# Routed expert blocks: the up product with the weights stationary, ScalarE copying each block's weights

## The chip, the cores and the metric

The kernel runs on one core of a Trainium2 chip. The metric is the time of one execution on the device in microseconds (us), as the median of several runs; lower is better.

## The reference

One decoder layer on x of shape (4, 512, 256), all in float32. Each of its three parts is fed by a layer norm and added to x: a selective state-space block of 2 layers, cross attention with 16 heads over a context of 512 rows, and a feed-forward part with 8 routed experts and a shared one. The change touches the last:

```python
xt = x.reshape(T, D)                      # T = 2048, D = 256
probs = softmax(xt @ Wg)                  # 8 experts
topv, topi = top_k(probs, 2); topv = topv / sum(topv)
cw = zeros((T, E)).at[arange(T)[:, None], topi].set(topv)
h = gelu(einsum('td,edf->tef', xt, Wu))   # F = 512
y = einsum('tef,efd->ted', h, Wd)
moe = einsum('ted,te->td', y, cw)
shared = gelu(xt @ W1) @ W2
out = x + shared + moe
```

## The kernel before

It is written engine by engine: for each stage a function per engine (pe_ffn, act_ffn, dve_ffn, pool_ffn, sp_ffn) issues that engine's instructions in a fixed order, and semaphores tie them together. An engine stops at a wait, and all that is queued behind it stops too. The state-space stage takes the span to about 1050 us and attention to about 1410 us; the feed-forward stage is the rest.

In the feed-forward stage the normed tokens xm are stored to x_hat in DRAM and transposed into xn; the router's logits, the softmax and the top two follow. Each of the 4096 choices of a token gets a row in one of NBLK = 39 blocks of 128 rows, and each block belongs to one expert. block_at holds for each block where the weights of its expert begin in w_up and w_down. The shared expert is worked out for all tokens, the first batch's output before the routed blocks and the others behind them (L1562).

The routed blocks run through this loop, in turns j:

- POOL gathers the 128 rows of a block from x_hat into xb (6 buffers) by an indirect DMA (pool_fetch, L1745), and scatters finished rows to y_choice by another (pool_send, L1751). Its queue holds fetch(j + 5), then send(j), then fetch(j + 6). A send waits until DVE has scaled the block.
- PE (L1552 to L1561) in turn j: the up product of block j (pe_up, L1501), the transposes of the rows of block j + 2 (pe_rows, L1495), the transposes of the hidden block j - 1 (pe_hidden_turn, L1510) and the down product of block j - 2 (pe_down, L1516). In pe_up the rows xt, 128x128 for each half of the model's width, are the stationary operand and 512 columns of w_up the moving one, so that the hidden block comes out with its rows on partitions. The down product needs the inner layer on partitions, hence the transposes.
- ACT applies Gelu from PSUM to hb (L1589).
- DVE in turn j: it scales the down product of block j - 3 by the gates into yb (dve_block_out, L1700), copies the transposed rows of j + 2 to xt (dve_rows, L1692) and the transposed hidden block of j - 1 to ht (dve_hidden, L1696).

In PSUM the up product has banks 0 and 1, the hidden transposes 2 and 3, the down product 4 and 5, the row transposes 6 and 7. When all scatters have landed, SP loads y_choice back (into w_up's place), DVE adds the two choices of every token to the residual (L1715), and the output is stored.

A float32 matmul leaves two weight loads and two matmuls in the trace, a transpose one of each; these are called passes here.

Of the kernel before, what the change touches and what calls it, by code (L numbers as in the profile page):

```python
# [8 lines left out]
ACT = mybir.ActivationFunctionType  # L9
# [6 lines left out]
P = 128  # L16
# [8 lines left out]
EXPERTS = 8  # L25
# [7 lines left out]
NBLK = 39  # L33
# [14 lines left out]
def build(nc, d, out):  # L48
# [14 lines left out]
    with ExitStack() as ctx:  # L63
# [5 lines left out]
        def sb(c, name, shape, dt=F32):  # L69
            return c.enter_context(nc.sbuf_tensor(name, shape, dt))  # L70
# [1267 lines left out]
        with ExitStack() as fc:  # L1338
# [28 lines left out]
            block_at = sb(fc, "block_at", [P, NBLK], I32)  # L1367
            NXB, NXT, NHT, NYB = 6, 3, 3, 4
            xb = sb(fc, "xb", [P, NXB, D])
            xt = sb(fc, "xt", [P, NXT, KD, P])  # L1370
            hb = sb(fc, "hb", [P, 2, F])
            ht = sb(fc, "ht", [P, NHT, FT, P])
# [25 lines left out]
            NHID, OUT0, RANKS, LOGITS = 4, 4, 6, 7  # L1398
            U0, H0, T0 = 0, 2, 6
            NTR = B * KD  # L1400
# [11 lines left out]
            fetched = [sem(f"fetched{n}") for n in range(NXB)]  # L1412
            xt_full, xt_out, up_full, up_act, ht_full, ht_out, y_full2, y_out2 = (
                sem(n) for n in ("xt_full", "xt_out", "up_full", "up_act", "ht_full", "ht_out", "y_full2", "y_out2"))
            sent = [sem(f"sent{n}") for n in range(NYB)]
# [84 lines left out]

            def pe_up(j, at):  # L1501
                pe.wait_ge(xt_out, j + 1)
                if j == 0:
                    pe.wait_ge(ld_up, 16 * EXPERTS)
                    pe.wait_ge(hid_act, NTR + NSH)
                for kt in range(KD):
                    m = pe.matmul(psum[:, U0 + j % 2, :], xt[:, j % NXT, kt, :], w_up[:, bass.ds(at + kt * F, F)], start=kt == 0, stop=kt == KD - 1)  # L1507
                m.then_inc(up_full, 1)

            def pe_hidden_turn(j):  # L1510
                pe.wait_ge(up_act, j + 1)
                for ft in range(FT):
                    m = pe.transpose(psum[:, H0 + j % 2, ft * P:(ft + 1) * P], hb[:, j % 2, ft * P:(ft + 1) * P], ident[:])
                m.then_inc(ht_full, 1)

            def pe_down(j, at):  # L1516
                pe.wait_ge(ht_out, j + 1)
                if j == 0:
                    pe.wait_ge(ld_down, 16 * EXPERTS)
                    pe.wait_ge(out_added, NEAR_OUT)  # L1520
                for ft in range(FT):
                    m = pe.matmul(out_bank(j)[:, 0:D], ht[:, j % NHT, ft, :], w_down[:, bass.ds(at + ft * D, D)], start=ft == 0, stop=ft == FT - 1)  # L1522
                m.then_inc(y_full2, 1)

            def pe_ffn():
# [26 lines left out]
                for j in range(NBLK + 2):  # L1552
                    if j < NBLK:
                        at[j] = pe.value_load(block_at[0:1, j:j + 1], min_val=0, max_val=(EXPERTS - 1) * KD * F)
                        pe_up(j, at[j])
                    if j + 2 < NBLK:
                        pe_rows(j + 2)
                    if 1 <= j <= NBLK:
                        pe_hidden_turn(j - 1)
                    if j >= 2:  # L1560
                        pe_down(j - 2, at[j - 2])  # L1561
# [3 lines left out]
            def act_expert_logits(b):  # L1565
                act.wait_ge(lg_full, b + 1)
                act.copy(lgT[:, b, :], psum[0:EXPERTS, OUT0 + b % 2, :]).then_inc(lg_act, 1)

            def act_ffn():
# [10 lines left out]
                for b in range(B):  # L1580
                    for ft in range(FT):
                        q = NTR + b * FT + ft
                        act.wait_ge(hid_full, q + 1)
                        if b == B - 1 and ft == 0:
                            act.wait_ge(hat_set, 16 * B)
                        act.activation(hs[b][:, ft, :], hid_bank(q), ACT.Gelu).then_inc(hid_act, 1)
                for j in range(NBLK):
                    act.wait_ge(up_full, j + 1)
                    act.activation(hb[:, j % 2, :], psum[:, U0 + j % 2, :], ACT.Gelu).then_inc(up_act, 1)  # L1589

# [101 lines left out]
            def dve_rows(j):  # L1692
                dve.wait_ge(xt_full, j + 1)
                dve.tensor_copy(xt[:, j % NXT], psum[:, T0 + j % 2, 0:D].rearrange("p (k c) -> p k c", k=KD)).then_inc(xt_out, 1)

            def dve_hidden(j):  # L1696
                dve.wait_ge(ht_full, j + 1)
                dve.tensor_copy(ht[:, j % NHT], psum[:, H0 + j % 2, :].rearrange("p (k c) -> p k c", k=FT)).then_inc(ht_out, 1)

# [23 lines left out]
            def dve_ffn():  # L1723
# [9 lines left out]
                for j in range(NBLK + 3):  # L1733
                    if j >= 3:
                        dve_block_out(j - 3)
                    if j + 2 < NBLK:
                        dve_rows(j + 2)
                    if 1 <= j <= NBLK:
                        dve_hidden(j - 1)
                for b in range(NEAR, B):  # L1740
# [145 lines left out]
```

## Time and profile before

| what | value |
|---|---|
| median of 3 runs | 1656.67 us |
| lowest, highest | 1651.78, 1661.15 us |
| profiled execution | 1661.1 us |
| its span, first to last instruction | 1659.6 us |
| its mean granted TensorE clock | 0.965 |
| instructions | 24075 |

How to read it: the span is what the hardware profiler sees of one execution, and the profiled execution's own time is 1.5 us more. Starts and lengths are in us from the span's start, ns where marked. PE is TensorE's matmul, PEld its weight load, PEldq and PE's queue its sequencer, DVE VectorE, ACT ScalarE, POOL GpSimd, SP SyncE. Matmuls are pipelined and their ends are modelled, so the distance from start to start tells more than a duration. L1507 is line 1507 of the kernel.

### The profile page before, as it was taken

What the parts mean: (1) busy time and instruction counts of PE and PEld (TensorE: products, weight loads), DVE (VectorE), ACT (ScalarE), POOL (GpSimd) and SP (SyncE); (2) the same over time, 40 slices, a digit from 0 to 9 for tenths busy, and PEclk for the clock granted to TensorE, in tenths of its full rate; (3) what the DMA queues carried; (4) which work ended last, traced back from release to release, by engine and by line L of the source; (5) the groups of instructions that cost most, each with busy time, mean ns of one, the idle gap of its engine ahead of it and who ended that gap; (6) DMA issues with size and microseconds to landing.
All of it is one profiled execution on the core that took longest, in us unless ns stands there. A gap on an engine that the chain in (4) does not pass through costs nothing.

```text
span 1659.6 us, 24075 instructions
## 1 busy us (share of the span) xinstructions
PE 1518.3 (91%) x8994; PEld 1149.5 (69%) x8994; DVE 1181.8 (71%) x1912; ACT 826.8 (50%) x1183; POOL 1001.4 (60%) x818
## 2 busy tenths in 40 slices
PE   4689999999999999999999897768979897999997
PEld 2478878978978879879888897524434343477776
DVE  4389989879879889889888789467667672333334
ACT  3656556656656556656556444105546556411110
POOL 1469878979979969969969987651303000034441
PEclk8999999999999999999999999969989999999999
DMA  4000100101100100101101120245323200612225
GB/s 152 19 26 27 52 26 27 52 26 53 52 26 27 52 26 27 52 26 36 43 26 66 51 102 1 64 83 120 61 55 54 49 1 1 261 38 65 66 64 168
DMA packets 38050, 92.27 MB, mean 56 GB/s; under 512 B 9136, under 2 KB 21936, under 8 KB 33456
## 3 DMA queue, kind: packets, MB, share of 16 engines
q1 hardware_dynamic: 29328, 73.16, 13.9%
q0 software_dynamic: 7584, 16.53, 3.9%
q10 hardware_dynamic: 1024, 1.05, 0.3%
q8 instruction: 73, 1.20, 0.3%
q14 instruction: 41, 0.34, 0.1%
HBM read 64.36 MB, written 9.57 MB: 45 GB/s over the span
## 4 chain that ended last, share of the span: by engine, by line
PE 75%; DVE 14%; issue 4%; ACT 3%; POOL 1%; SPq 1%; DMA 1%; DVEq 0%; ACTq 0%; POOLq 0%
PE psum L491 23%; PE psum L472 10%; PE psum L423 5%; DVE uw L534 4%; PE psum L1522 4%; PE psum L1507 4%; DVE hst L632 4%; PE psum L1091 4%; PE psum L1073 2%; PE psum L452 2%; PE psum L1057 2%; ACT pT L1146 2%; PE psum L1452 2%; PE psum L1017 2%; PE psum L447 1%
## 5 line engine op out<-in xcount | busy, mean ns | idle before, releaser
L801 POOL TENSOR_TENSOR hst<-hst,cb 128x512 f32<-128x512 f32 x399 | 510.8, 1305 | 126.8 <-DVE hst L632 125.8
L632 DVE TENSOR_TENSOR_SCAN hst<-dA,hst,psum 128x256 f32<-128x256 f32 x399 | 277.0, 729 | 79.7 <-PE psum L491 78.0
L632 DVE TENSOR_TENSOR_SCAN hst<-dA,psum 128x256 f32<-128x256 f32 x399 | 253.0, 669 | 40.4 <-ACT dA L743 20.6
L491 PE MATMUL psum<-filt,uT 128*128 128x172 f32 (+1 forms) x1536 | 269.3, 312 | 11.3 <-DVE hst L632 9.1
L491 PE MATMUL psum<-filt,c_early 128*128 128x172 f32 (+1 forms) x1536 | 269.3, 312 | 9.1 <-DVE hst L632 5.9
L491 PEld LDWEIGHTS psum<-filt,c_early 128*128 128x128 f32 x1536 | 233.5, 192 | 47.0 <-issue 20.8
L491 PEld LDWEIGHTS psum<-filt,uT 128*128 128x128 f32 x1536 | 232.4, 191 | 40.4 <-DVE hst L632 15.2
L743 ACT ACTIVATE dA<-delta,alog 128x512 f32<-128x512 f32 x256 | 176.9, 721 | 152.4 <-DVE hst L632 121.5
L743 ACT ACTIVATE dA<-xres,alog 128x512 f32<-128x512 f32 x256 | 177.0, 720 | 127.6 <-DVE hst L632 100.0
L472 PE MATMUL psum<-ident,hst 128*128 128x128 f32 x1596 | 239.9, 274 | 0.0
L1218 DVE TENSOR_REDUCE nmax<-psum 128x2 f32<-128x1024 f32 x128 | 154.9, 1221 | 80.1 <-PE psum L1057 79.8
L472 PEld LDWEIGHTS psum<-ident,hst 128*128 128x128 f32 x1596 | 199.7, 141 | 1.1
L1146 ACT ACTIVATE pT<-psum 128x1024 f32<-128x1024 f32 x128 | 127.9, 1024 | 82.3 <-PE psum L1077 80.9
L801 POOL TENSOR_TENSOR w_early<-w_early,cb 128x512 f32<-128x512 f32 x113 | 145.9, 1307 | 29.9 <-DVE w_early L632 29.7
L1748 POOL DMA_INDIRECT xb<-x_hat,origin x39 | 37.9, 972 | 189.5 <-DVE c_early L1690 178.0
L423 PE MATMUL psum<-xnT,w_early 128*128 128x512 f32 x256 | 124.6, 614 | 4.0 <-DVE uw L534 2.8
L1301 POOL DMA_DIRECT2D qk<-part x72 | 34.5, 489 | 151.7 <-PE psum L1077 131.6
L780 POOL TENSOR_TENSOR filt<-toep,bcol 128x2064 f32<-128x2064 f32 x32 | 116.9, 3654 | 0.0
L632 DVE TENSOR_TENSOR_SCAN w_early<-dA,w_early,psum 128x256 f32<-128x256 f32 x113 | 80.1, 729 | 25.6 <-PE psum L491 25.3
L1589 ACT ACTIVATE hb<-psum 128x512 f32<-128x512 f32 x39 | 23.3, 598 | 145.7 <-PE psum L1507 129.0
L1057 PE MATMUL psum<-qk 64*128 64x512 f32 x256 | 59.9, 470 | 38.2 <-DMA qk<-part 15.4
L1754 POOL DMA_INDIRECT y_choice<-yb,goal x39 | 38.6, 989 | 79.7 <-DVE yb L1706 79.7
(217 smaller groups left out, 2313.4 us busy)
## 6 DMA issues: line engine op xcount, KB each, us to landing
cb<-c_rows SPq DMA_DIRECT2D x32, 1024.0 KB, 4.6
qk<-part SPq DMA_DIRECT2D x120, 64.0 KB, 2.5
qk<-part POOLq DMA_DIRECT2D x72, 64.0 KB, 4.8
w_up<-up_dram SPq DMA_DIRECT2D x8, 512.0 KB, 7.8
w_down<-down_dram SPq DMA_DIRECT2D x8, 512.0 KB, 14.0
w_up<-y_choice SPq DMA_DIRECT2D x8, 512.0 KB, 7.9
xm<-x_dram SPq DMA_DIRECT2D x4, 512.0 KB, 7.8
w_early<-w_in_dram SPq DMA_DIRECT2D x2, 1024.0 KB, 5.5
```

The source lines that it names most:

```text
L423: i = pe.matmul(bk, w_in[:, kt, m8 * P:(m8 + 1) * P], xnT[:, kt, :], start=kt == 0, stop=kt == KD - 1)
L472: m = pe.matmul(psum[:, Y0 + et, t * P:(t + 1) * P], hst(i)[:, t * P:(t + 1) * P], ident[:], start=n == 0 and t == 0, stop=n == NSTATE - 1 ...
L491: m = pe.matmul(bk[:, :, t0:t0 + width], uT[k % 2][:, c, et * P:(et + 1) * P], filt[:, f % 2, c, n2:n2 + 2, 0:width], start=True, stop=True)
L534: i = dve.scalar_tensor_tensor(out=dst, in0=bk[:, 0:S - late], scalar=w_cv[:, l, j, tap:tap + 1], in1=dst, op0=ALU.mult, op1=ALU.add)
L632: dve.tensor_tensor_scan(h[:, t0:t0 + HS], dA[:, st % NDA, t0:t0 + HS], bank("v", i)[:, n * HS:(n + 1) * HS], h[:, t0 - 1:t0] if t0 else 0 ...
L743: act.activation(dA[:, a % NDA, :], delta[k % 2][:, et, :], ACT.Exp, scale=alog[:, k // B, et, n:n + 1]).then_inc(decay_done, 1)
L780: pool.tensor_tensor(filt[:, f % 2], toep[:, :].unsqueeze(1).unsqueeze(1).to_broadcast([P, NCH, GN, QC]), bcol[:, k % 2, :, g * GN:(g + 1) ...
L801: pool.tensor_tensor(h, h, cb[:, q % 2, state_of(i)[1] % GN, :], ALU.mult).then_inc(g_done, 1)
L1057: m = pe.matmul(o[:, e, :], qk[k0:k0 + KR, b % 2, 0, j, half, t * P:(t + 1) * P], qk[k0:k0 + KR, b % 2, 1, j, half, :], start=True, stop=T ...
L1091: m = pe.matmul(psum[i * HROW:(i + 1) * HROW, PV, :], vt[:, cp, kv, c0:c0 + HROW], pT[:, (m0 + i // 2) % NPT, i % 2, :], start=kv == 0, st ...
L1146: act.activation(pT[:, m % NPT], pair(u, "score", s), ACT.Exp, scale=HDIM ** -0.5).then_inc(pair_act, 1)
L1218: dve.tensor_reduce(nmax[:, u % 2, t, 2 * j:2 * j + 2], pair(u, "max", r), AX.X, ALU.max, negate=True).then_inc(pair_dve, 1)
```

## The change

The up product is turned round: the expert's weights become the stationary operand, 128x128 at a time (4 tiles of the inner layer by 2 halves of the model's width), and the 128 rows of the block the moving one. It comes out with the inner layer on partitions, as the down product wants it. The transposes of the hidden block (pe_hidden_turn) and DVE's copy (dve_hidden) are gone, and ACT's Gelu writes ht itself. For each block ACT reads block_at into a register and copies the 128x1024 weights of its expert from w_up to one of 4 fixed places, wu, which lie in xn's memory (act_weights); it does so for block j + 1 ahead of the Gelu of block j. The up product now has 4 PSUM banks (NUB = 4). New waits: the up product for the copy and for the Gelu of 4 blocks before, the down product for DVE's scaling of 2 blocks before, the Gelu for the down product of 3 blocks before, dve_rows for the up product of 3 blocks before.

```diff
--- before.py
+++ after.py
@@ -1365,10 +1365,10 @@
             passed = sb(fc, "passed", [P, NBLK, EXPERTS])
             blockf = sb(fc, "blockf", [P, NBLK])
             block_at = sb(fc, "block_at", [P, NBLK], I32)
-            NXB, NXT, NHT, NYB = 6, 3, 3, 4
+            NXB, NXT, NHT, NYB, NWU = 6, 3, 3, 4, 4
             xb = sb(fc, "xb", [P, NXB, D])
+            wu = xn[:].rearrange("p b k s -> p (b k s)").rearrange("p (n c) -> p n c", n=NWU)
             xt = sb(fc, "xt", [P, NXT, KD, P])
-            hb = sb(fc, "hb", [P, 2, F])
             ht = sb(fc, "ht", [P, NHT, FT, P])
             yb = sb(fc, "yb", [P, NYB, D])
             NSEND = 2 * TOPK * NT
@@ -1396,7 +1396,8 @@
             token_no = route_c[:, 576:576 + NT]
 
             NHID, OUT0, RANKS, LOGITS = 4, 4, 6, 7
-            U0, H0, T0 = 0, 2, 6
+            U0, NUB, T0 = 0, 4, 6
+            wu_set = sem("wu_set")
             NTR = B * KD
             NSH = B * FT
             NGO = TOPK * NT
@@ -1410,8 +1411,8 @@
                 sem(n) for n in ("choice_dve", "gate_dve", "place_dve", "hot_dve", "goal_dve", "blocks_set", "goals_set"))
             hat_set = sem("hat_set")
             fetched = [sem(f"fetched{n}") for n in range(NXB)]
-            xt_full, xt_out, up_full, up_act, ht_full, ht_out, y_full2, y_out2 = (
-                sem(n) for n in ("xt_full", "xt_out", "up_full", "up_act", "ht_full", "ht_out", "y_full2", "y_out2"))
+            xt_full, xt_out, up_full, ht_out, y_full2, y_out2 = (
+                sem(n) for n in ("xt_full", "xt_out", "up_full", "ht_out", "y_full2", "y_out2"))
             sent = [sem(f"sent{n}") for n in range(NYB)]
             y_loaded, y_summed = [sem(f"y_loaded{b}") for b in range(B)], sem("y_summed")
 
@@ -1498,23 +1499,23 @@
                     m = pe.transpose(psum[:, T0 + j % 2, kt * P:(kt + 1) * P], xb[:, j % NXB, kt * P:(kt + 1) * P], ident[:])
                 m.then_inc(xt_full, 1)
 
-            def pe_up(j, at):
+            def pe_up(j):
                 pe.wait_ge(xt_out, j + 1)
+                pe.wait_ge(wu_set, j + 1)
                 if j == 0:
-                    pe.wait_ge(ld_up, 16 * EXPERTS)
                     pe.wait_ge(hid_act, NTR + NSH)
-                for kt in range(KD):
-                    m = pe.matmul(psum[:, U0 + j % 2, :], xt[:, j % NXT, kt, :], w_up[:, bass.ds(at + kt * F, F)], start=kt == 0, stop=kt == KD - 1)
+                if j >= NUB:
+                    pe.wait_ge(ht_out, j - NUB + 1)
+                for ft in range(FT):
+                    for kt in range(KD):
+                        m = pe.matmul(psum[:, U0 + j % NUB, ft * P:(ft + 1) * P], wu[:, j % NWU, kt * F + ft * P:kt * F + (ft + 1) * P], xt[:, j % NXT, kt, :],
+                                      start=kt == 0, stop=kt == KD - 1)
                 m.then_inc(up_full, 1)
-
-            def pe_hidden_turn(j):
-                pe.wait_ge(up_act, j + 1)
-                for ft in range(FT):
-                    m = pe.transpose(psum[:, H0 + j % 2, ft * P:(ft + 1) * P], hb[:, j % 2, ft * P:(ft + 1) * P], ident[:])
-                m.then_inc(ht_full, 1)
 
             def pe_down(j, at):
                 pe.wait_ge(ht_out, j + 1)
+                if j >= 2:
+                    pe.wait_ge(y_out2, j - 1)
                 if j == 0:
                     pe.wait_ge(ld_down, 16 * EXPERTS)
                     pe.wait_ge(out_added, NEAR_OUT)
@@ -1552,11 +1553,9 @@
                 for j in range(NBLK + 2):
                     if j < NBLK:
                         at[j] = pe.value_load(block_at[0:1, j:j + 1], min_val=0, max_val=(EXPERTS - 1) * KD * F)
-                        pe_up(j, at[j])
+                        pe_up(j)
                     if j + 2 < NBLK:
                         pe_rows(j + 2)
-                    if 1 <= j <= NBLK:
-                        pe_hidden_turn(j - 1)
                     if j >= 2:
                         pe_down(j - 2, at[j - 2])
                 for b in range(NEAR, B):
@@ -1565,6 +1564,12 @@
             def act_expert_logits(b):
                 act.wait_ge(lg_full, b + 1)
                 act.copy(lgT[:, b, :], psum[0:EXPERTS, OUT0 + b % 2, :]).then_inc(lg_act, 1)
+
+            def act_weights(j):
+                at = act.value_load(block_at[0:1, j:j + 1], min_val=0, max_val=(EXPERTS - 1) * KD * F)
+                if j >= NWU:
+                    act.wait_ge(up_full, j - NWU + 1)
+                act.copy(wu[:, j % NWU, :], w_up[:, bass.ds(at, KD * F)]).then_inc(wu_set, 1)
 
             def act_ffn():
                 for b in range(B):
@@ -1584,9 +1589,16 @@
                         if b == B - 1 and ft == 0:
                             act.wait_ge(hat_set, 16 * B)
                         act.activation(hs[b][:, ft, :], hid_bank(q), ACT.Gelu).then_inc(hid_act, 1)
+                act.wait_ge(blocks_set, 1)
+                act.wait_ge(ld_up, 16 * EXPERTS)
+                act_weights(0)
                 for j in range(NBLK):
+                    if j + 1 < NBLK:
+                        act_weights(j + 1)
                     act.wait_ge(up_full, j + 1)
-                    act.activation(hb[:, j % 2, :], psum[:, U0 + j % 2, :], ACT.Gelu).then_inc(up_act, 1)
+                    if j >= NHT:
+                        act.wait_ge(y_full2, j - NHT + 1)
+                    act.activation(ht[:, j % NHT], psum[:, U0 + j % NUB, :].rearrange("p (k c) -> p k c", k=FT), ACT.Gelu).then_inc(ht_out, 1)
 
             def dve_route_choose():
                 lg = psum[:, LOGITS, 0:NT * EXPERTS].rearrange("p (t x) -> p t x", x=EXPERTS)
@@ -1691,11 +1703,9 @@
 
             def dve_rows(j):
                 dve.wait_ge(xt_full, j + 1)
+                if j >= NXT:
+                    dve.wait_ge(up_full, j - NXT + 1)
                 dve.tensor_copy(xt[:, j % NXT], psum[:, T0 + j % 2, 0:D].rearrange("p (k c) -> p k c", k=KD)).then_inc(xt_out, 1)
-
-            def dve_hidden(j):
-                dve.wait_ge(ht_full, j + 1)
-                dve.tensor_copy(ht[:, j % NHT], psum[:, H0 + j % 2, :].rearrange("p (k c) -> p k c", k=FT)).then_inc(ht_out, 1)
 
             def dve_block_out(j):
                 dve.wait_ge(y_full2, j + 1)
@@ -1735,8 +1745,6 @@
                         dve_block_out(j - 3)
                     if j + 2 < NBLK:
                         dve_rows(j + 2)
-                    if 1 <= j <= NBLK:
-                        dve_hidden(j - 1)
                 for b in range(NEAR, B):
                     dve_outputs_late(b)
                     dve_choices(b - 1)
```

## Rows read from the trace of the kernel before

**Rows 1.** The page's first part: busy time, share of span, instructions of each engine

```profile
PE 1518.3 (91%) x8994; PEld 1149.5 (69%) x8994; DVE 1181.8 (71%) x1912; ACT 826.8 (50%) x1183; POOL 1001.4 (60%) x818
```

**Rows 2.** Busy time of each engine in 40 us of the routed blocks

```profile
core 0: us, PE busy (x) PEld busy (x) DVE busy (x) ACT busy (x) POOL busy (x), PEclk, DMA share, GB/s
1480.00:1520.00 40.00, 40.00 (x179) 28.29 (x178) 15.52 (x29) 5.98 (x10) 19.68 (x20) 1.00 0.19 63
```

**Rows 3.** The chain of waits from 1440 us to the end, by line

```profile
by line: PE psum L1522 30.6%; PE psum L1507 30.5%; PE psum L1436 9.4%; PE psum L1513 7.7%; PE psum L1452 6.8%; PE psum L1498 3.7%; PE psum L1492 3.2%; PE psum L1462 3.2%; DVE xres L1715 1.7%; issue 0.9%; DVE xres L1730 0.3%; DVE xt L1694 0.
```

**Rows 4.** Timeline, one turn: start us, us, engine, line, operation, count [idle before]

```profile
1520.09 1.88 PE L1507 MATMUL psum<-w_up,xt 128*128 x4
1520.29 0.48 DVE L1706 TENSOR_SCALAR yb<-psum,c_early 128x256 f32<-128x256 f32 x1 [1.04 <-PE psum L1522]
...
1521.05 0.99 POOL L1754 DMA_INDIRECT y_choice<-yb,goal  x1 [1.83 <-DVE yb L1706]
...
1521.80 0.38 PE L1498 MATMUL psum<-ident,xb 128*128 128x128 f32 x2
...
1522.02 0.60 PE L1513 MATMUL psum<-ident,hb 128*128 128x128 f32 x4
...
1522.35 0.97 POOL L1748 DMA_INDIRECT xb<-x_hat,origin  x1 [0.30 <-PE psum L1498]
...
1522.46 1.89 PE L1522 MATMUL psum<-w_down,ht 128*128 x8
1522.66 0.69 DVE L1698 COPY ht<-psum 128x512 f32<-128x512 f32 x1
...
1524.19 1.88 PE L1507 MATMUL psum<-w_up,xt 128*128 x4
...
1525.87 0.20 PEld L1498 LDWEIGHTS psum<-ident,xb 128*128 128x128 f32 x2 [0.63 <-DMA xb<-x_hat,origin]
```

**Rows 5.** Gathered rows xb, 1480 to 1620 us: time to landing, and PE's waits

```profile
DMA to landing us min/median/max: 2.7/2.7/3.3
...
PEld psum L1498 <- DMA xb<-x_hat,origin: 2.4, 5, 0.6
```

**Rows 6.** Timeline of PE where float32 matmuls of 128 columns stand

```profile
1440.96 0.38 PE L1486 MATMUL psum<-member,route_c 128*128 128x128 f32 x2
1441.18 0.39 PE L1487 MATMUL psum<-member,route_c 128*128 128x128 f32 x2
1441.40 1.02 PE L1452 MATMUL psum<-xn,raw 128*128 128x512 f32 x2
```

**Rows 7.** L1492, 78 columns: its weight loads (ns min/median/max), then its matmuls' timeline

```profile
L1492 PEld LDWEIGHTS psum<-c_early,w_early x64: 186/192/192, 1454.9 to 1462.1; 128*128 128x128 f32 x64
...
1455.14 7.27 PE L1492 MATMUL psum<-c_early,w_early 128*128 128x78 f32 x64
```

**Rows 8.** Groups of ScalarE: busy us, mean ns | idle before

```profile
L1146 ACT ACTIVATE pT<-psum 128x1024 f32<-128x1024 f32 x128 | 127.9, 1024 | 82.3 <-PE psum L1077 80.9
L743 ACT ACT_TABLE_LOAD x19 | 24.4, 1283 | 0.3
...
L1574 ACT COPY xn<-psum 128x512 f32<-128x512 f32 x8 | 4.5, 588 | 3.5 <-PE psum L1531 3.5
```

**Rows 9.** PE's queue reads a block's register: ns min/median/max, first and last start

```profile
L1554 PEldq TENSOR_LOAD <-block_at x39: 297/301/491, 1468.4 to 1618.2; - x39
...
L1554 PEldq SEQ_ASSERT  x39: 18/18/32, 1469.2 to 1618.8; - x39
```

**Rows 10.** Timeline where the routed blocks begin

```profile
1470.56 1.98 PE L1507 MATMUL psum<-w_up,xt 128*128 x4 [0.76 <-DVE xt L1694]
...
1472.57 0.60 ACT L1589 ACTIVATE hb<-psum 128x512 f32<-128x512 f32 x1 [16.63 <-issue]
```

**Rows 11.** Timeline of the tail

```profile
1644.00 7.07 PE L1436 MATMUL psum<-raw,xm 128*128 128x256 f32 x32
...
1651.71 4.87 DVE L1715 TENSOR_TENSOR xres<-xres,w_up 128x1024 f32<-128x1024 f32 x4
```

## Prediction

> **What bounds the kernel now.** The core's totals come first: TensorE is busy for 91% of the span, more than any other engine [rows 1]. That is an average over stages, so the next view is the table by stretch, for the stage that the change touches, the 39 routed blocks [rows 2]. In 40 us there PE is busy 40.00 us, POOL 19.68, DVE 15.52 and ACT 5.98, at a granted clock of 1.00 (2.4 GHz). A busy PE can still hide waits, as the ends of its matmuls are modelled, so two more views are needed. The chain of waits from 1440 us on says the same: nearly all of its 220 us are PE lines, the up product L1507 30.5%, the down product L1522 30.6%, the hidden transposes L1513 7.7% and the row transposes L1498 3.7%, against 0.9% of issue [rows 3]. The timeline of one turn of the loop shows how little is between them [rows 4]: the up product starts at 1520.09, the row transposes at 1521.80, the hidden ones at 1522.02, the down product at 1522.46 and the next up product at 1524.19. A turn is 4.10 us and divides into 1.71 (up, 4 passes), 0.22 (2 transposes), 0.44 (4 transposes) and 1.73 (down, 8 passes). I read starts, not durations: a pass of 512 columns has its next start after 0.43 us and the transposes follow at 0.11 us. So each microsecond taken out of PE's stream in a turn comes off the stage, until something else is late.
>
> What could be late next is the gather of rows. After the down product's end (1520.09) follow DVE's scaling (1520.29), POOL's scatter (1521.05) and, behind it in the same queue, POOL's gather of the rows that PE transposes in the next turn (1522.35) [rows 4]. It lands 2.7 us after its issue, 3.3 at worst [rows 5], say 1525.05, and PE needs it at the end of the next up product, 1525.90. Five gathers in 140 us (34 blocks) came after PE's weight load could have started, 2.4 us in all and 0.6 the longest; the one in this turn let the load start at 1525.87, which is still before the up product's end [rows 4, 5].
>
> **The change, part by part.**
>
> *Hidden transposes and DVE's copy go.* 4 passes, 0.44 us from 1522.02 to 1522.46 [rows 4], for 39 blocks: 17.0 us off the path. The chain gives the same: 7.7% of 220 us is 16.9, 0.109 a pass [rows 3]. DVE loses its copy L1698 (0.69 us a turn, rows 4), and ACT's hop through hb becomes a direct write of ht. Neither is late now, so both count as nothing.
>
> *The up product is turned round.* Now xt is the stationary operand: 2 matmuls of 512 columns, each two passes (x4 in rows 4), 1.71 us. Afterwards the weights are: 4 x 2 matmuls of 128 columns, 16 passes, each with its own load of 128x128 weights. Columns times passes are the same, 2048; the question is what a pass of 128 columns costs when each needs a new load. L1486 and L1487 are exactly such matmuls, float32, 128x128 weights, 128 columns, two passes each: they start at 1440.96 and 1441.18, and the next line at 1441.40, so 0.110 us a pass [rows 6]. Bounds: the transposes' 0.109 [rows 3], and the 64 passes back to back of L1492, which move only 78 columns and so are held by the load, 7.27 us or 0.1136 a pass [rows 7]. I take 0.110: 16 x 0.110 = 1.76 us, 0.045 more than now, 39 blocks +1.8 us; bounds +1.1 and +4.0.
>
> The Trainium skill, "TensorE: Matmul & The Clock Gate", section "Part 3: Packing small matmuls — row/col tiling", says that a weight load overlaps matmuls in flight only when it goes to other row groups. The trace disagrees: these loads use all 128 rows, and they follow each other at 0.11 us though one lasts 0.19 [rows 7]. By that rule the sum would turn positive, which is the last rival below.
>
> *The row transposes and the down product stay.* 0.22 and 1.73 us. The new turn is 1.76 + 0.22 + 1.73 = 3.71 us.
>
> *ScalarE copies weights.* Per block one read of the block's place into a register and one copy of 128x1024 from SBUF to SBUF. The copy is not in the trace; nearest are the activation of 128x1024 from PSUM, 1.02 us, and the table load of 1.28 us as a far upper end [rows 8]. I take 1.0. The same register read on PE's queue spans 1468.4 to 1469.2, some 0.8 us and up to 1.1 with what follows it [rows 9]. With the Gelu (0.60, rows 10) and 0.2 for a wait, ACT needs 2.9 of 3.71 us a turn, and the copy for block j+1 is queued ahead of the Gelu of block j, right behind the Gelu of j-1, so it is finished some 2.2 us after the up product of j-1 and due 3.71 + 0.22 + 1.73 = 5.66 us after it. Cover: 0.8 us of idle ACT a turn, and that lead of 3.4 us. What waits behind the copy on ACT is the Gelu, whose result PE wants two turns later. Cost nothing in the steady loop. At the start the first two turns have no down product (1.98 us each), and the copy for block 2 is issued after the Gelu of block 0: 1472.57 + 1.0 + 1.0 + 0.2 = 1474.8, against an up product due at 1470.56 + 3.96 = 1474.52 [rows 10]. That is +0.3 us once (bounds 0 and 1). The copies for blocks 0 and 1 are hidden: ACT is idle before block 0's Gelu at 1472.57 for 16.63 us [rows 10].
>
> *Added waits.* The down product of j waits for DVE's scaling of j-2, the up product for the Gelu of j-4, DVE's xt copy for the up product of j-3. Each event lies about a turn or more back (the scaling is done 0.7 us after its product, rows 4), so nothing. PE still reads its block register for the down product; the read (0.30 us, rows 9) and what depends on it must fit under the down product's 1.73 us, which it does.
>
> *The gather comes closer.* Unchanged chain: from the down product's end to landing 1525.05 - 1520.09 = 4.96 us, some 5.05 until PE can act, and 5.78 in the late case (1525.87 - 1520.09). What PE leaves it shrinks from 4.10 + 1.71 = 5.81 to 3.71 + 1.76 = 5.47 us. The median still fits, by 0.4; a late one costs 0.3. A wait of 0.63 now would cost 0.31, so about 0.3 of each stays hidden: 2.4 - 5 x 0.3 = 0.9 us together. Bounds: nothing, and 39 x 0.31 = 12 us if each landed like the worst.
>
> *Head and tail.* Before block 0, PE is held by the chain to the gathered rows, which stays. In the tail PE's late shared outputs run on to about 1651, and only then come DVE's last sums at 1651.71 [rows 11]; the scatter's and y_back's chain starts from the last down product too. So the saving shifts the whole tail.
>
> **Sum.** -17.0 + 1.8 + 0.3 + 0.9 = -14.0 us. The profiled execution took 1661.1 us (span 1659.6), so its like would be 1647.1. It is the slowest of the runs shown, 4.4 us above their median; against the median, 1656.67 - 14.0 = 1642.7 us, -0.84%.
>
> **The rivals.**
>
> *The gather sets the turn.* If landings move up by 0.4 us or more (gather and scatter share one queue, and now come every 3.7 us), the turn is landing time less the up product: with the late 5.78 each time, 5.78 - 1.76 = 4.02 us, a gain of 0.08 x 39 = 3 us, 1654. Halfway, 5.6: 3.84 a turn, gain 10. For it: five late ones of 34. Against it: the median is 2.7 us and so is the least, so the bulk is tight; POOL is at work 20 of 40 us and stays below 22 [rows 2, 5]. Chance of a gain under 8 us through this or dearer passes: 0.12.
>
> *ScalarE becomes the bound (slower).* If copy and Gelu each needed a table load, ACT would have 2 x 1.28 + 1.0 + 0.6 + 1.0 + 0.2 = 5.4 us a turn, and it decides from 3.71 on: 39 x (5.4 - 4.1) = +51, 1708 us. Against it: L1574's copies come after Sqrt work and show no load at their line, while loads stand with the Exp of L743 [rows 8]. The Trainium skill, "ScalarE: Activation LUTs", "Table sets: the hidden batching unit", says that copy is in every set; the trace agrees. Chance 0.04.
>
> *Weight loads don't overlap (slower).* A pass is then load (0.19, rows 7) and stream (0.11, rows 6), 0.30 us: up 4.8 us, turn 6.75, +103 us, 1760. Rows 6 and 7 speak against it; what is new is only that 16 stand together and that the weights differ from those there. Chance 0.02.
>
> *The change does less than it says.* PE might grant less clock in the stage, or its queue might run dry in the stream of short passes. 64 short passes ran at 0.11 us each, and the routed stage with its short transposes has a clock of 1.00 [rows 2, 7]. Chance 0.02, somewhere near no change.
>
> **How the numbers follow.** Forecast 0.80 (gains of 10 to 17 us): 1642.7. The runs before lie 9.4 us apart, so a median can miss by some 4. The range goes from a gain of 17 with 4 of scatter (1636) to a gain of 7 with 4 of scatter (1654). About 0.5%, 8.3 us, is what a measurement can tell from no change. Faster: 0.80; within 0.5%: 0.13; slower: 0.07.
>
> **What would show it.** Turns of 3.7 us between down products; L1513 and L1698 gone; up passes at 0.11 us start to start; a copy of about 1.0 us on ACT with no table loads in the loop; PE's weight load for the row transposes waiting for the gather in a few turns only, by about 0.3 us; the tail the same length. Wrong would be: a wait for the gather in most turns, passes over 0.12 us, or PE waiting for the weights' copy after block 2.

## The result, and the profile after

| | before | changed |
|---|---|---|
| median of 7 runs | 1653.58 us | 1644.12 us |
| lowest to highest | 1651.78 to 1661.15 | 1641.13 to 1647.13 |
| ratio of changed to before | | 0.993 (95%: 0.9914 to 0.9946) |
| span of the profiled execution | 1659.6 us | 1641.0 us |
| routed stage in it, first up product to late shared outputs | 159.63 us | 149.83 us |
| from there to the end of the span | 29.4 us | 29.4 us |

The change makes the kernel faster, by 0.7% or 11.6 us (8.9 to 14.2); the two medians lie 9.5 us apart. The two profiled spans differ by 18.6 us, but half of that is not the change's: block 0's up product starts at 1470.56 before [rows 10] and at 1461.83 after, and ahead of it both kernels do the same work. In the twelve kernels below that start lies anywhere between 1461.3 and 1472.0 us. So the stage is what to compare between traces, and the ratio over many runs for the whole. The stage's ends after, in the timeline:

```profile
1461.83 2.05 PE L1511 MATMUL psum<-xt,xn 128*128 128x128 f32 x16 [0.68 <-DVE xt L1708]
...
1611.66 4.70 PE L1437 MATMUL psum<-raw,hs_own 128*128 128x256 f32 x21
```

The late shared outputs start at 1611.66, against 1630.19 before. 1611.66 - 1461.83 = 149.83 us, 9.8 less than before, which lies within the ratio's interval.

The page's totals and the 40 us inside the stage (the views of rows 1 and 2; columns as there):

```profile
PE 1497.7 (91%) x9306; PEld 1169.9 (71%) x9306; DVE 1154.9 (70%) x1873; ACT 866.9 (53%) x1222; POOL 1001.0 (61%) x818
```

```profile
core 0: us, PE busy (x) PEld busy (x) DVE busy (x) ACT busy (x) POOL busy (x), PEclk, DMA share, GB/s
1480.00:1520.00 40.00, 39.07 (x268) 36.49 (x267) 9.51 (x21) 16.61 (x21) 20.13 (x21) 1.00 0.21 67
```

PE stays the bound; of 40 us it now stands still for 0.93, ACT's busy time rises from 5.98 to 16.61 us with the copies, DVE's falls from 15.52 to 9.51, and the clock stays at 1.00 [rows 2]. The chain of waits from 1435 us on (the view of rows 3) has a new entry:

```profile
by line: PE psum L1511 27.9%; PE psum L1523 26.9%; DMA xb<-x_hat,origin 12.8%; PE psum L1437 10.1%; PE psum L1453 5.8%; PE psum L1499 4.7%; PE psum L1493 3.4%; PE psum L1463 3.4%; DVE xres L1725 1.8%; issue 1.3%; DVE xres L1740 0.3%; DVE xt
```

The hidden transposes' 7.7% are gone, and the gathered rows, which did not show before, hold 12.8%: the chain runs through a gather wherever PE waited for one. A turn without such a wait (the view of rows 4):

```profile
1469.80 1.95 PE L1511 MATMUL psum<-xt,xn 128*128 128x128 f32 x16
1470.01 0.48 DVE L1716 TENSOR_SCALAR yb<-psum,c_early 128x256 f32<-128x256 f32 x1 [1.31 <-PE psum L1523]
1470.78 1.00 POOL L1762 DMA_INDIRECT y_choice<-yb,goal  x1 [7.77 <-DVE yb L1716]
...
1471.59 0.38 PE L1499 MATMUL psum<-ident,xb 128*128 128x128 f32 x2
1471.79 0.60 ACT L1601 ACTIVATE ht<-psum 128x512 f32<-128x512 f32 x1 [2.05 <-PE psum L1511]
1471.81 1.89 PE L1523 MATMUL psum<-w_down,ht 128*128 x8
...
1472.08 0.98 POOL L1756 DMA_INDIRECT xb<-x_hat,origin  x1 [0.30 <-PE psum L1499]
1472.42 1.04 ACT L1572 COPY xn<-w_up 128x1024 f32 x1
1473.54 1.95 PE L1511 MATMUL psum<-xt,xn 128*128 128x128 f32 x16
```

From 1469.80 to 1473.54 a turn is 3.74 us by these rows, 3.73 in the median: up product 1.79, row transposes 0.22, down product 1.73. The Gelu starts 0.20 us after the up product's end and the copy of the weights directly behind it. And a turn with a wait:

```profile
1477.27 1.95 PE L1511 MATMUL psum<-xt,xn 128*128 128x128 f32 x16
...
1479.25 0.60 ACT L1601 ACTIVATE ht<-psum 128x512 f32<-128x512 f32 x1 [2.06 <-PE psum L1511]
1479.54 0.97 POOL L1756 DMA_INDIRECT xb<-x_hat,origin  x1 [0.30 <-issue]
1479.74 0.20 PEld L1499 LDWEIGHTS psum<-ident,xb 128*128 128x128 f32 x2 [0.72 <-DMA xb<-x_hat,origin]
...
1480.02 1.92 PE L1523 MATMUL psum<-w_down,ht 128*128 x8
...
1481.78 1.95 PE L1511 MATMUL psum<-xt,xn 128*128 128x128 f32 x16
```

The row transposes would have followed the up product at 1477.27 + 1.79 = 1479.06, but their weight load waited for the gather until 1479.74; the turn takes 4.51 us. In the whole stage, PE's waits for the gather (us in all, times, longest) are:

```profile
PEld psum L1499 <- DMA xb<-x_hat,origin: 4.1, 7, 0.7
PE psum L1499 <- DMA xb<-x_hat,origin: 2.8, 7, 0.5
```

The two lines belong together: in seven turns the weight load, then the matmul, was held by the same gather. Those turns are 4.51, 4.47, 4.42, 4.33, 4.46, 4.18 and 4.25 us long, 4.5 us over seven of 3.73. (One of 3.81, the third, makes 4.6.)

### The profile page after: what moved, and what is told of

The parts are those of the page before. It is cut to its first block, busy times and chain, and to the rows that moved or that the text cites. A ratio compares the mean times of both kernels' runs of the same rounds, so it can differ in the third digit from the quotient of the medians.

```text
span 1641.0 us, 24925 instructions
## 1 busy us (share of the span) xinstructions
PE 1497.7 (91%) x9306; PEld 1169.9 (71%) x9306; DVE 1154.9 (70%) x1873; ACT 866.9 (53%) x1222; POOL 1001.0 (61%) x818
## 3 DMA queue, kind: packets, MB, share of 16 engines
q1 hardware_dynamic: 29328, 73.16, 14.2%
## 4 chain that ended last, share of the span: by engine, by line
PE 74%; DVE 14%; issue 4%; ACT 4%; DMA 3%; SPq 1%; POOL 0%; DVEq 0%; ACTq 0%; POOLq 0%
PE psum L491 24%; PE psum L472 11%; PE psum L423 6%; DVE uw L534 4%; DVE hst L632 4%; PE psum L1091 4%; PE psum L1511 4%; PE psum L1523 3%; PE psum L1073 2%; PE psum L452 2%; ACT pT L1146 2%; PE psum L1057 2%; PE psum L1453 2%; DMA xb<-x_hat,origin 2%; PE psum L1017 1%
## 5 line engine op out<-in xcount | busy, mean ns | idle before, releaser
L423 PEld LDWEIGHTS psum<-xnT,w_early 128*128 128x128 f32 x256 | 45.8, 197 | 46.4 <-issue 37.0
## 6 DMA issues: line engine op xcount, KB each, us to landing
w_down<-down_dram SPq DMA_DIRECT2D x8, 512.0 KB, 14.2
```

Of the source, the lines that this page charges most:

```text
L423: i = pe.matmul(bk, w_in[:, kt, m8 * P:(m8 + 1) * P], xnT[:, kt, :], start=kt == 0, stop=kt == KD - 1)
```

## The experiments

Each kernel is the changed one or the one before with one edit. "The stage" is measured as above.

**Where do the late gathers come from?** In the changed kernel they stand in turns 5, 10, 14, 18, 22, 31 and 35. The DMA queues show what runs beside the gathers (packets, MB, share of 16 engines). Before, from 1476 to 1630 us:

```profile
q8 instruction: 6, 0.10, 0.3%
q14 instruction: 1, 0.01, 0.0%
```

and after, from 1470 to 1611 us:

```profile
q8 instruction: 9, 0.15, 0.5%
q14 instruction: 3, 0.02, 0.1%
```

These packets carry the engines' own instructions. Those of 16 KB, in q8, I take for PE's: PE has 52 loads and matmuls in a turn where it had 36, and they come once in 4.3 turns where they came once in 5.6. In turn 4 such a packet of 16 KB is under way from 1477.07 on, 1.26 us after the gather's issue at 1475.81; the queues from 1477.0 to 1477.5:

```profile
q8 instruction: 1, 0.02, 15.9%
q0 software_dynamic: 2, 0.01, 8.5%
```

That gather is the one which PE waits for in turn 5. The first three kernels move the loop in PE's instruction stream without changing its work:

```diff
 def pe_ffn():
+    for _ in range(8):        # 16 and 24 in the two others
+        pe.transpose(psum[:, RANKS, 400:401], ident[0:1, :], ident[0:1, 0:1])
```

> The changed kernel with 16 more PE instructions (8 tiny transposes of one row) put where PE idles before the feed-forward stage: the routed loop is the same work, only its place in PE's instruction stream moves by 16. In the changed kernel PE waits for a late gather in 7 of 39 turns, nearly always 4 turns apart, 4.5 us in all, and each time a packet of PE's own instructions (16 KB, once in 4 turns) runs about 1.3 us behind the gather's issue. Theory (the instruction packet holds up the gather): the packets move against the turn by a quarter of its instructions, the late gathers become other ones, more or fewer, and the stage from the first up product to the late shared outputs (149.8 us in the changed kernel) comes out between 145.0 and 152; in at least one of the three shifts there are at most 2 late gathers and the stage is under 146.5. Rival (scatter and gather in one queue disturb each other every four blocks by themselves, at the new shorter turn): 7 late turns 4 apart and 149.8 +-0.5 in all three shifts.

```profile
PEld psum L1499 <- DMA xb<-x_hat,origin: 3.6, 7, 0.8
PE psum L1499 <- DMA xb<-x_hat,origin: 2.1, 6, 0.6
```

Stage 149.18 us, 7 late turns: 6, 9, 13, 22, 26, 31, 34.

> As e1_shift16 with 32 instructions, half a turn's. Theory of the instruction packets: they now run half a turn's instructions away from where they hit, most likely ahead of the gather's issue, where those of the kernel before did no harm: few late gathers, stage 145.0 to 147. Rival of the shared queue: 149.8 +-0.5 with 7 late turns.

```profile
PEld psum L1499 <- DMA xb<-x_hat,origin: 3.3, 8, 0.5
PE psum L1499 <- DMA xb<-x_hat,origin: 1.7, 6, 0.4
```

Stage 148.96 us, 8 late turns: 5, 9, 13, 17, 22, 26, 30, 34.

> As e1_shift16 with 48 instructions, three quarters of a turn's. Theory of the instruction packets: another count of late gathers than 7, stage between 145.0 and 152. Rival of the shared queue: 149.8 +-0.5 with 7 late turns.

```profile
PEld psum L1499 <- DMA xb<-x_hat,origin: 3.1, 6, 0.9
PE psum L1499 <- DMA xb<-x_hat,origin: 1.9, 5, 0.7
```

Stage 148.63 us, 6 late turns: 5, 9, 21, 26, 30, 34.

Neither side came out as written. The late turns move and their number changes, which the rival of two transfers disturbing each other every four blocks did not allow. But no shift got rid of them: the packets do not spread over the turn as I expected, most of them still start 3.5 to 3.7 us into it, about 1.4 us after the gather's issue. What the traces do show is that lateness and packets go together. Over the six kernels with 6 buffers and the turned product (these three, the changed kernel, e9 and e10) I count 44 turns over 3.78 us from turn 3 on and 48 packets of 16 KB. Each of the 44 has a packet that started after 2.3 us of the turn before, or within the first 0.4 us of the late turn itself. The four packets that did no harm started 2.4 to 3.0 us into their turn.

The next kernel adds instruction packets by another engine, whose work nobody waits for in the stage:

```diff
+for j in range(NBLK):
+    for _ in range(128):     # two waits go into one instruction
+        sp.wait_ge(up_full, j + 1)
 for n in range(NYB):
     sp.wait_ge(sent[n], 16 * len(range(n, NBLK, NYB)))
```

> The changed kernel with 64 more instructions for SP per block, waits that are met already: PE, ACT, DVE, POOL and every transfer of data stay as they are, and only SP's own instructions have to be fetched as well. Theory (a packet of instructions on the DMA engines holds up the gather that runs with it): 6 to 10 more instruction packets in the stage, and with them more late gathers, 10 to 17 of 39 turns instead of 7; stage 149.8 + 2 to 6 = 152 to 156 us. Rival (packets and late gathers only share a cause, such as PE's place in its loop): 6 to 8 late turns, stage 148.6 to 150.

```profile
PEld psum L1499 <- DMA xb<-x_hat,origin: 4.9, 8, 0.8
PE psum L1499 <- DMA xb<-x_hat,origin: 3.3, 7, 0.6
```

Stage 150.77 us, 8 late turns. (SP could not keep up with its 64 instructions a block and went on long after the others, so the whole kernel's 1746.8 us mean nothing here.) In the stage its packets came to six, of 8 KB; five started 0.6 to 2.5 us into the turn, where the harmful ones hardly start, and the sixth after the last gather. No late turn goes with one of them alone. Eight late turns are what the rival had, the stage is above its 150 us and below the theory's 152, and the run does not decide: the packets were fewer, smaller and elsewhere than planned.

**What a packet does to a gather.** The traces also hold the DMA packets, each with its start, and they settle more than these four kernels. A gather of 128 rows is 32 packets of 4 KB with data and 16 of 4 bytes that report them, and it has landed with the last report. This is the end of the gather that PE waits for in turn 5, issued at 1475.81, from 1478.2 to 1479.3:

```profile
q0 software_dynamic: 3, 0.01, 5.0%
```

and the same part of the next one's flight, issued at 1479.54 and on time, from 1481.92 to 1483.0:

```profile
q0 software_dynamic: 2, 0.00, 0.1%
```

The next gather has no data left by then, only two reports. The late one still has two packets of data and a report; the two start at 1478.33 and 1478.75, and the instruction packet ended at 1477.07 + 1.27 = 1478.34. In each of the seven late gathers the last data but one starts within 0.02 us of the instruction packet's end. So the packet holds up one pair of the gather's 32 packets, not the gather as a whole; that both stand in the queue of the same DMA engine is an inference, as the trace does not name the engine.

The fourteen kernels together say the same, from turn 2 on. 330 of 455 gathers have no instruction packet in flight with them (one that starts in the last microsecond before the landing is not counted); they land 2.5 to 2.9 us after their issue, none later. All 76 that land after more than 2.95 us have one, 71 of 16 KB and 5 of 8 KB. What decides is when the 16 KB packet ends. In 26 cases it was over by 1.2 us after the gather's issue, and those gathers landed after 2.6 to 2.8 us; in five it ended up to 1.5 us after, and they landed after 2.7 to 3.0. In the other 70 it ended 1.6 us or more after the issue, and those landed after 3.0 to 4.3 us, always 1.2 to 1.5 us after the packet's end. This holds where no engine waits for a gather, so the lateness is not an effect of PE's wait: in e5_xb8 below, five gathers are late by this measure and none is waited for. In e8_copy4 below all eight packets start 0.55 to 0.7 us before a gather's issue, and every gather is on time:

```profile
DMA to landing us min/median/max: 2.6/2.7/2.8
```

It also answers why e9 did no more harm: SP's five packets were over before or soon after a gather's issue. No kernel was run without instruction packets, so this is shown by the order and distance of events and not by taking the packets away.

Open is what sets the moment of the fetch, and so why shifting the code did not move most packets. With e5's buffers they start 1.4 to 3.1 us into the turn, in e8, where PE waits for ScalarE's copy, 0.9 to 1.0 us. A fetch that is tied to the place where PE waits would fit; it was not tried.

**What do the late gathers cost?** More buffers let POOL issue each gather earlier.

```diff
-NXB, NXT, NHT, NYB, NWU = 6, 3, 3, 4, 4
+NXB, NXT, NHT, NYB, NWU = 8, 3, 3, 4, 4
```

> The changed kernel with 8 buffers for gathered rows in place of 6, so that each gather is issued two turns earlier. Theory (late gathers cost the changed kernel 4.5 us, whatever makes them late): no wait for a gather in the loop, turns of 3.73 us throughout, stage 149.8 - 4.5 = 145.3 us; against the kernel before a ratio of 0.9901 to 0.9905, 0.0027 better than the change alone (0.993). Rival (the longer turns come from something else, such as PE's own instruction supply): stage and ratio as with the change alone.

```profile
DMA to landing us min/median/max: 2.6/2.8/3.5
```

Stage 145.20 us; every turn from the third on is 3.73 us and there is no line of a wait for the gather. The landing stays between 2.6 and 3.5 us: gathers still come late, and the two turns of lead cover it. 149.83 - 145.20 = 4.6 us is what the late ones cost. The ratio against the kernel before is 0.9916 (0.9893 to 0.9939): clearly faster than before, but the step from the change alone, 0.993, is smaller than both intervals, so it rests on the traces.

The same in the kernel before (hb = xn[:, 0] makes the room):

> The kernel before with 8 buffers for gathered rows (hb moved into the free place of xn to make room). Theory (there the late gathers were hidden under the longer turn): stage 159.6 +-0.2 us as before, ratio 1.000. Rival (they cost there as well, so that the change did not bring them): 1 to 3 us less.

Stage 159.60 us, ratio 0.9987 (0.9969 to 1.0004). The late gathers of rows 5 cost nothing there, as the timeline had it.

One more buffer instead of two:

> The changed kernel with 7 buffers for gathered rows, one more than it has. Theory (a gather is at most 0.8 us late, and one buffer more gives it a whole turn of 3.73 us): no waits for a gather, stage 145.2 us and ratio 0.9916 against the kernel before, as with 8. Rival (a longer queue of transfers is what helped with 8): stage between 146 and 149.

Ratio 0.9923 (0.9909 to 0.9937). There is no wait for a gather here either, and all turns from the fourth on are 3.73 us. The stage is 146.74 us all the same, because of one event in its head, which belongs to neither theory:

```profile
1465.28 1.95 PE L1511 MATMUL psum<-xt,xn 128*128 128x128 f32 x16
...
1466.93 0.60 ACT L1601 ACTIVATE ht<-psum 128x512 f32<-128x512 f32 x1 [15.35 <-remote]
1466.98 0.93 DVE L1708 COPY xt<-psum 128x256 f32<-128x256 f32 x2 [3.53 <-remote]
...
1468.74 2.02 PE L1511 MATMUL psum<-xt,xn 128*128 128x128 f32 x16 [1.30 <-ACT xn L1572]
```

ACT and DVE both start only at 1466.9, though the up product had ended at about 1465.0, and the trace gives what they waited for only as "remote"; turn 1 takes 3.47 us instead of 2.0. Without it the stage would be 145.3. The same event shows in e10 (turn 1 of 3.11 us) and e11 (4.9, and 7.1 in turn 2), not in the other kernels. What it is stays open.

**What do the four transposes bring?** They are added again, without use, ahead of the row transposes, into the free half of their bank:

```diff
 pe.wait_ge(fetched[j % NXB], 16 * (j // NXB + 1))
+for n in range(4):
+    pe.transpose(psum[:, T0 + j % 2, (2 + n % 2) * P:(3 + n % 2) * P], xb[:, j % NXB, n % 2 * P:(n % 2 + 1) * P], ident[:])
```

> The changed kernel with 4 transposes a turn added again, their result unused, ahead of the row transposes. Theory (PE's stream sets the turn, 4 short passes are worth 0.44 us, and a gather that is 0.7 us late is hidden again when the turn is 0.44 longer): turn 3.73 + 0.44 = 4.17 us, +17.1 us, less the 4.5 us of waits for late gathers of which at most 1.5 stay: stage 149.8 + 17.1 - 3 to 4.5 = 162.4 to 164. Rival (the gather's chain sets the stage, PE has room): the stage grows by under 8 us, to at most 158.

```profile
1501.24 0.60 PE L1499 MATMUL psum<-ident,xb 128*128 128x128 f32 x4
...
1501.67 0.38 PE L1501 MATMUL psum<-ident,xb 128*128 128x128 f32 x2
1501.89 1.89 PE L1525 MATMUL psum<-w_down,ht 128*128 x8
...
1503.62 1.95 PE L1513 MATMUL psum<-xt,xn 128*128 128x128 f32 x16
...
1507.79 1.95 PE L1513 MATMUL psum<-xt,xn 128*128 128x128 f32 x16
```

From up product to up product, 1503.62 to 1507.79, a turn is 4.17 us: 0.44 more for the four passes of L1499 (1501.24 to 1501.67). Stage 162.44 us, at the lower end of what was expected. 37 turns have the additions: +16.1; the waits for late gathers shrink from 4.6 to 1.1: -3.5; together +12.6, as measured.

**What holds a pass of the up product?**

```diff
-psum[:, U0 + j % NUB, ft * P:(ft + 1) * P], ..., xt[:, j % NXT, kt, :]
+psum[:, U0 + j % NUB, ft * P:ft * P + 64], ..., xt[:, j % NXT, kt, 0:64]
```

> The changed kernel with 8 buffers for gathered rows (so without late gathers, turns of 3.73 us), in which the up product is worked out for 64 of a block's 128 rows only; the other half of each hidden block is left out. Theory A (a pass is held by its load of 128x128 weights, as L1492 with its 78 columns at 0.1136 us a pass was): a pass still takes 0.110 to 0.114 us, turn 3.70 to 3.75. Theory B (a pass is held by its columns): 0.056 us a pass, 16 x 0.056 = 0.9 us less, turn 2.8 to 2.9, unless the gather sets it, then 3.3 at most.

```profile
1522.15 1.89 PE L1511 MATMUL psum<-xt,xn 128*128 128x64 f32 x16
...
1523.88 0.39 PE L1499 MATMUL psum<-ident,xb 128*128 128x128 f32 x2
...
1524.11 1.25 PE L1523 MATMUL psum<-w_down,ht 128*128 x5
```

The row transposes start 1.73 us after the up product, 0.108 us a pass, against 1.79 us and 0.112 with 128 columns; the turn is 3.68 us. Half the columns save 0.05 us of 1.79. So at 128 columns and below the columns do not set a pass; a price that comes with each load and matmul does, about 0.11 us. The product could be turned round at 0.07 us a block because 128 columns, a quarter of the 0.43 us that 512 take, ask for just as much. That this price is the load's own is likely, as every pass here has a new load, but no kernel keeps its weights for short passes, so it is not shown. Theory A's turn of 3.70 to 3.75 is missed by 0.02 us.

**Is the copy on ScalarE free?** First alone, in the kernel before (the up product still moves 512 columns, from wu):

> The kernel before with ScalarE's copy of the weights alone: the up product still moves 512 columns of weights and holds the rows, now from the copied place. Theory (ScalarE has the time, and nobody waits for the copy): stage 159.6 +-0.3 us, ratio 1.000. Rival (the copy costs something, by SBUF traffic or by holding up the Gelu): stage over 161 us.

Stage 159.60 us, ratio 1.0001 (0.9987 to 1.0016): it is. Then repeated, into a place that nobody reads:

```diff
 if j >= NWU:
     act.wait_ge(up_full, j - NWU + 1)
+for n in range(3):            # 1 in e10_copy2, with 1 * j in the wait
+    if j or n:
+        act.wait_ge(dumped, 3 * j + n)
+    act.copy(dump_w[:], w_up[:, bass.ds(at, KD * F)]).then_inc(dumped, 1)
 act.copy(wu[:, j % NWU, :], w_up[:, bass.ds(at, KD * F)]).then_inc(wu_set, 1)
```

> The changed kernel with each block's weights copied four times by ScalarE, three of them to an unused place. Theory (the copy is free only while ScalarE's own turn is under PE's 3.73 us): ScalarE needs Gelu 0.60 + 4 x 1.04 + about 0.2 = 4.95 us a turn and becomes the bound, turns of 4.9 to 5.2 us, no waits for gathers, stage 145.3 + 38 x 1.2 = 191 us (186 to 200). Rival (the lead of the copies hides even this): under 155 us.

```profile
1522.37 1.04 ACT L1577 COPY xn<-w_up 128x1024 f32 x1
1523.32 0.59 ACT L1606 ACTIVATE ht<-psum 128x512 f32<-128x512 f32 x1
1523.51 2.02 PE L1512 MATMUL psum<-xt,xn 128*128 128x128 f32 x16 [0.57 <-issue]
1523.81 3.19 ACT L1576 COPY dump_w<-w_up 128x1024 f32 x3
...
1526.91 1.04 ACT L1577 COPY xn<-w_up 128x1024 f32 x1
1527.86 0.59 ACT L1606 ACTIVATE ht<-psum 128x512 f32<-128x512 f32 x1
```

ACT is busy without a gap, 4.54 us from Gelu to Gelu, and PE's up product waits until the last copy is written (1522.37 + 1.04 = 1523.41). ScalarE is the bound, so the point from which it decides is real, but the turn is 4.53 us and not 4.95, the stage 177.22 us and not 186 or more. The starts tell why. After the Gelu at 1523.32 the copies start at 1523.81, 1524.88, 1525.96 and 1526.91 and the next Gelu at 1527.86: steps of 0.49, 1.07, 1.08, 0.95 and 0.95 us. The second and third copy wait for the one before them, as they write the same place, and cost 1.07 and 1.08; an instruction that waits for nothing starts 0.10 us before the record of the one ahead ends (0.49 after a Gelu recorded as 0.59, 0.95 after a copy recorded as 1.04). The 0.2 us that I had set for a wait are not there. The split 0.59 + 4 x 0.95 + 0.14, which the next expectation uses, has the right sum and the wrong parts.

> The changed kernel with each block's weights copied twice by ScalarE, once to an unused place. With four copies a turn was 4.53 us = 0.59 for the Gelu + 4 x 0.95 from copy to copy + 0.14. Theory (nothing until ScalarE's turn passes PE's 3.73 us): 0.59 + 2 x 0.95 + 0.14 = 2.63 us, no change: median turn 3.73, stage 148.5 to 150. Rival (the copies already cost something in proportion): median turn above 3.75.

Median turn 3.73 us, as expected; the stage, 150.80 us, is over what I gave by 0.8, with late gathers of 4.5 us as in the changed kernel and the head event's 1.1 us. Two copies start 0.95 us apart there, too. A second copy costs the loop nothing.

## Why the prediction was right, and where a term was off

The forecast was -14.0 us or -0.84%; measured are 11.6 us (8.9 to 14.2) over the runs and 9.8 in the stage. That the forecast of 1642.7 us lies 1.4 from the measured median of 1644.12 is in part luck: the gain between the medians, 9.5, was put 4.5 us too high, and the starting point, 1656.67 where seven runs give 1653.58, 3.1 too high as well. Point by point:

- *What bounds the stage.* Right: PE's stream. Four passes taken out shorten the turn by 0.44 us, and four put back (e4) lengthen it by 0.44.
- *Hidden transposes, -17.0.* Right; e4 gives 0.436 us a turn.
- *The up product turned round, +1.8 (1.1 to 4.0).* Measured: 1.78 us for 16 passes (3.73 less 0.22 and 1.73) against 1.71, so 39 x 0.07 = +2.7 us, 0.112 a pass, between the row that I took and L1492's. e11 shows why L1492 with its 78 columns was a fair row for it: with 64 columns a pass still takes 0.108 us. The Trainium skill's rule that a load overlaps matmuls in flight only when it goes to other row groups ("TensorE: Matmul & The Clock Gate", "Part 3: Packing small matmuls — row/col tiling") does not hold in this trace: loads of 0.19 us follow each other at 0.11. The same section elsewhere also lets a load to a background weight buffer run ahead, which the prediction left out and which the trace would fit.
- *ScalarE's copy, nothing but +0.3 at the start.* Right for the loop (e7, e10). The copy lasts 1.04 us by its record. No table load stands in the loop. The Trainium skill ("ScalarE: Activation LUTs", "Table sets: the hidden batching unit") has copy in every table set, and the trace agrees. At the start, turns 0 and 1 took 2.11 and 2.06 us where 1.98 was set: +0.2.
- *The wait for late gathers, +0.9 (0 to 12).* This is the term that was off: 4.6 us. The mechanism was named and its place, but not its size. I took the waits seen before and let 0.3 of each be hidden. Both factors changed: there are 7 late ones instead of 5, and each is later: from issue to PE's load 1479.74 - 1475.81 = 3.93 us, where the worst before was 1525.87 - 1522.35 = 3.52 [rows 4]. I treated the lateness as a property of the gather. It comes from the packets of instructions, and the change adds to just these: 9 packets of 16 KB in the windows shown instead of 6. They also meet the gathers later in their flight. Before, the four harmful ones started 0.6 to 0.9 us after the issue and the gathers landed after 3.1 to 3.5 us; in the changed kernel the seven started 1.3 to 1.4 us after it, and the gathers landed after 3.6 to 3.9.
- *Added waits, head, tail.* Nothing, as said; the tail is 29.4 us in both.

The sum with measured terms: -17.0 + 2.7 + 0.2 + 4.6 = -9.5, against 9.8 in the stage. Of the rivals, the gather setting the turn came true in seven turns and not in the other thirty; had it been so in all, e5 would have brought more than 4.6 us.

## What to carry to other kernels

When a stage is bound by one engine's stream, count passes and their start-to-start distance; which operand is stationary cost little here, where the moving one still had 128 columns a pass (with 64 a pass took hardly less). Taking work off the stream also takes away cover: list the transfers that were late and hidden, and give them another buffer in the same edit (here 4.6 of the 14.4 us that both bring together, by the stages). Compare stages, not spans, where the code ahead of the stage can move its start by 10 us from one execution to the next.

## What the runs showed of the hardware that I had not expected

- A float32 pass with a new load of 128x128 weights takes 0.112 us with 128 columns and 0.108 with 64.
- A ScalarE copy of 128x1024 float32 within SBUF is recorded as 1.04 us, but one that waits for nothing starts 0.95 us after the copy ahead of it, and one that waits for that copy 1.07 (e8).
- Packets of instructions, 16 KB each and most likely PE's, run on the DMA engines about once in four turns here. Two of a gather's 32 data packets can wait for one: in the changed kernel the waiting data starts within 0.02 us of the packet's end, and over all kernels a gather whose packet ends 1.6 us or more after its issue lands 1.2 to 1.5 us after that end, after up to 4.3 us instead of 2.7. A packet that is over by 1.2 us after the issue does nothing.
